# Stored input product of the r and z gates added on TensorE instead of VectorE, in a GRU followed by routed experts

## The chip, the cores and the metric

The kernel runs on one core of a Trainium2 chip. The metric is the device time of one execution, in microseconds (us). PE is TensorE (products; PEld its weight loads), DVE is VectorE, ACT is ScalarE, POOL is GpSimd, SP issues most transfers.

## The reference

A GRU with 512 units runs over 512 time steps for 4 sequences; its states are the input of a two-of-four mixture of experts, and the result is added to x. In the excerpt the expert part is cut, since the change does not touch it.

```python
def cell(h, x):
    gi = x @ W_ih + b_ih
    gh = h @ W_hh + b_hh
    i_r, i_z, i_n = jnp.split(gi, 3, axis=-1)
    h_r, h_z, h_n = jnp.split(gh, 3, axis=-1)
    r = jax.nn.sigmoid(i_r + h_r)
    z = jax.nn.sigmoid(i_z + h_z)
    n = jnp.tanh(i_n + r * h_n)
    h_new = (1.0 - z) * n + z * h
    return (h_new, h_new)
...
_, hs = jax.lax.scan(cell, initial_state, xs)
...
x = x + _L0_ffn_ref(hs, Wg, bg, W1, W2)
```

## The kernel before

**Segments.** Each sequence is cut into 16 segments of L = 32 steps, so 4 x 16 = 64 columns (COLS) run side by side. The start of a segment is found by running the 40 steps ahead of it from zero: 8 steps (BURN) on the end of the segment before the last one, then 32 on the last one. After 8 and after 40 steps the states are shifted by one segment (L985 `shift`), and the first column gets the true initial state. Then 32 steps follow whose states are kept. That makes FIRST + L = 72 steps. A test on DVE (L1053 `check`) compares each segment's end with the start that the next one assumed; if the largest gap is above 2^-20 of the largest state, all engines run 32 steps more, up to 15 times.

**Numbers.** Weights and states are scaled by powers of two and split into an fp16 high half and an fp16 low half. The first 20 steps (ROUGH) multiply high by high only: 4 k-tiles x 4 units x 3 gates = 48 products of 128x128 by 128x64. The other 52 are exact and take high x high, high x low weight and low state x high: 144 products. A "unit" j is one of four blocks of 128 hidden units; its three gates r, z, n lie in PSUM bank j.

**The input product** gi = x W_ih is made in four chunks of 8 steps. The first is made before step 0 in fp32 (L319, 12 tiles in 4 banks, each emptied by ACT at L545 or L548). The other three are made beside the steps, as "fills": 18 split products of 512 columns (L336) per step in steps 0 to 23 (FILLED), 1.5 tiles a step, emptied by ACT (L554) into fp32 in SBUF. The order in a rough step is 13 fills, the first k-tile, 2 fills, and so on (FILLS). From step 24 on a step has no fills.

**One step.** PE waits for the high half of state tile k (`high_ready`) and, once per unit, until the bank is read (`rn_done`). For each unit DVE adds the r and z part of gi to PSUM (L934 `pre_rz`), ACT takes one sigmoid of both (L582), POOL forms z h (L720), DVE forms r (h_n + b) (L939 `reset`), adds i_n (L944), ACT takes tanh (L587), DVE forms (z - 1) n (L948), then the new state's high half (L955 `blend`) and, again in fp32, the state itself (L960, L965). In exact steps POOL forms the low halves 0 to 2 (L728), DVE the last one (L970). The orders are written out by hand: `ORDER` (L225) for PE, `exact` and `rough` (L972, L976) for DVE, L589 for ACT. Between steps DVE also splits x and W_hh (L878, L925), one piece per step.

**Start-up.** DVE takes maxima of W_ih (L854), x (L862) and W_hh (L884), POOL reduces them over partitions (L702 to L708), DVE makes power-of-two scales of them (L840 `pow2`), ACT and DVE split W_ih (L528, L873). The first six tiles are kept unscaled and multiplied later (L909).

## Time and profile before

| what | value |
|---|---|
| runs, us | 954.76, 973.03, 952.18 |
| median, us | 954.76 |
| the profiled execution, us | 953.15 |
| its span, first to last instruction, us | 951.4 |
| granted PE clock, mean over the span | 0.955 |
| busy share PE, DVE, ACT, POOL | 84%, 70%, 44%, 21% |

The span is one profiled execution; it is 1.75 us shorter than that execution's own time. A timeline row has its start, its length from the first start to the last end, engine, line, operation, what is written and read, the number of instructions merged into it, and in brackets the idle time before it with what ended it. A "mean ns" of a product is its own latency; products overlap, so rates are taken from starts.

### The profile page before, as it was taken

To read this page: it belongs to the slowest core of one execution; us is meant where nothing else is said; L and a number is where in the kernel's file an instruction comes from. 1 tells how busy PE (TensorE), PEld (TensorE's weight loads), DVE (VectorE), ACT (ScalarE), POOL (GpSimd) and SP (SyncE) were. 2 spreads that over 40 slices of the span, in tenths; PEclk is the share of its full clock that TensorE was granted. 3 is DMA by queue.
4 is the path that set the end of the run, shared out by engine and by line. 5 is a ranking of instruction groups with operands and counts; after the bars stand their busy time and mean duration, and the time that the engine had idled before them with its cause. 6 is when DMAs were issued, how large, how long until landed. Compare 5 with 4: busy or idle time off the path is not lost.

```text
span 951.4 us, 27392 instructions
## 1 busy us (share of the span) xinstructions
PE 798.6 (84%) x11202; PEld 516.0 (54%) x11203; DVE 664.7 (70%) x2254; ACT 419.8 (44%) x844; POOL 195.8 (21%) x507
## 2 busy tenths in 40 slices
PE   6998788998888688887884514899999999999996
PEld 2444444577777677777774513444444444444442
DVE  5867777767888788888885586567765767575500
ACT  1656455654444344444442330574175418334700
POOL 1012111233333333333331001001201210210011
PEclk9999999999999999999997855999999999999999
DMA  9700000000000000000002274053525523370012
GB/s 346 273 2 2 1 2 2 2 3 3 4 3 4 2 4 3 4 3 4 4 3 90 91 221 165 14 180 85 167 61 171 154 67 132 90 208 12 1 18 27
DMA packets 20162, 62.52 MB, mean 66 GB/s; under 512 B 2064, under 2 KB 2064, under 8 KB 17424
## 3 DMA queue, kind: packets, MB, share of 16 engines
q1 hardware_dynamic: 15744, 52.46, 15.8%
q0 software_dynamic: 3584, 8.42, 5.0%
q8 instruction: 81, 1.33, 0.6%
q14 instruction: 33, 0.27, 0.1%
q10 hardware_dynamic: 720, 0.03, 0.0%
HBM read 52.49 MB, written 12.62 MB: 68 GB/s over the span
## 4 chain that ended last, share of the span: by engine, by line
PE 69%; DVE 20%; issue 5%; ACT 4%; DMA 1%; POOL 0%; DVEq 0%; POOLq 0%; SPq 0%; ACTq 0%
PE ps L344 21%; PE ps L486 17%; PE ps L499 17%; DVE wa L934 5%; PE ps L319 5%; DVE wa L939 4%; PE ps L336 3%; DVE wa L944 3%; DVE halves L955 3%; PE ps L428 2%; DVE ocand L948 2%; ACT wa L582 2%; PE ps L466 1%; DMA big<-in_w_ih 1%; PE ps L474 1%
## 5 line engine op out<-in xcount | busy, mean ns | idle before, releaser
L344 PE MATMUL ps<-halves,wa 128*128 128x64 f16 x8448 | 292.0, 194 | 76.6 <-DVE halves L955 66.4
L344 PEld LDWEIGHTS ps<-halves,wa 128*128 128x128 f16 x8448 | 272.2, 98 | 115.7 <-DVE wa L939 56.3
L582 ACT ACTIVATE wa<-wa,un_gates 128x128 f32<-128x128 f32 x288 | 112.6, 398 | 163.5 <-DVE wa L934 155.1
L486 PE MATMUL ps<-wb,big 128*128 128x512 f16 x768 | 166.9, 379 | 1.6 <-DVE wb L1246 1.6
L499 PE MATMUL ps<-big 128*128 128x512 f16 x768 | 166.9, 379 | 0.0
L486 PEld LDWEIGHTS ps<-wb,big 128*128 128x128 f16 x768 | 74.8, 98 | 91.6 <-issue 1.8
L587 ACT ACTIVATE wa<-wa,un_gates 128x64 f32<-128x64 f32 x288 | 94.1, 343 | 67.9 <-DVE wa L944 65.6
L499 PEld LDWEIGHTS ps<-big 128*128 128x128 f16 x768 | 75.2, 98 | 89.9
L934 DVE TENSOR_TENSOR wa<-ps,big 128x128 f32<-128x128 f32 x288 | 81.1, 287 | 54.0 <-PE ps L344 54.0
L336 PE MATMUL ps<-hx,wb 128*128 128x512 f16 x432 | 109.8, 386 | 0.0
L647 ACT ACTIVATE hx<-ps,un_hid_in 128x512 f32<-128x512 f32 x64 | 43.7, 683 | 112.5 <-PE ps L486 110.2
L720 POOL TENSOR_TENSOR wa<-wa,carried 128x64 f32<-128x64 f32 x160 | 52.3, 331 | 167.8 <-ACT wa L582 165.5
L955 DVE SCALAR_TENSOR_TENSOR halves<-ocand,neg_scale,wa 128x64 f16<-128x64 f32 x288 | 80.8, 280 | 8.4 <-issue 0.6
L939 DVE SCALAR_TENSOR_TENSOR wa<-ps,bhn_s,wa 128x64 f32<-128x64 f32 x288 | 80.0, 278 | 5.6 <-ACT wa L582 5.5
L1138 DVE SCALAR_TENSOR_TENSOR big<-wa,scale,big 128x2048 f16<-128x2048 f32 x28 | 65.3, 2349 | 25.9 <-ACT big L633 25.9
L633 ACT ACTIVATE big<-wa,scale 128x2048 f16<-128x2048 f32 x32 | 62.5, 1989 | 44.6 <-DVEq L1126 44.6
L1259 DVE SCALAR_TENSOR_TENSOR big<-hx,hid_scale,big 128x512 f16<-128x512 f32 x64 | 47.9, 749 | 42.8 <-ACT big L650 36.6
L944 DVE TENSOR_TENSOR wa<-wa,big 128x64 f32<-128x64 f32 x288 | 69.7, 242 | 2.5
L1097 DVE TENSOR_REDUCE chunk_peak<-wa 128x1 f32<-128x2048 f32 x32 | 71.1, 2276 | 0.0
L948 DVE SCALAR_TENSOR_TENSOR ocand<-wa 128x64 f32<-128x64 f32 x288 | 62.8, 218 | 10.9 <-ACT wa L587 10.9
L720 POOL TENSOR_TENSOR wa<-wa,hx 128x64 f32<-128x64 f32 x128 | 41.4, 323 | 88.0 <-ACT wa L582 84.4
L778 POOL DMA_INDIRECT out<-hx,idx_out x16 | 29.1, 1818 | 136.1 <-DVE hx L1265 136.1
(168 smaller groups left out, 610.9 us busy)
## 6 DMA issues: line engine op xcount, KB each, us to landing
wa<-in_w SPq DMA_DIRECT2D x32, 1024.0 KB, 7.7
hs_rows<-big SPq DMA_DIRECT2D x8, 516.0 KB, 6.3
big<-in_w_ih SPq DMA_DIRECT2D x3, 1024.0 KB, 11.3
hx<-in_x_t SPq DMA_DIRECT2D x3, 1024.0 KB, 20.0
big<-in_w_hh SPq DMA_DIRECT2D x4, 768.0 KB, 16.4
wa<-in_x_t SPq DMA_DIRECT2D x1, 1024.0 KB, 4.9
hx<-hs_rows,idx POOLq DMA_INDIRECT x16
out<-hx,idx_out POOLq DMA_INDIRECT x16, 4.9
```

What stands on the lines that cost most here:

```text
L336: mm = pe.matmul(ps[:, 4 + tile % 4, :], wih_parts[:, w, k, m * P:(m + 1) * P], x_parts[:, q, t, k, :], start=(left == 0), stop=(left == K ...
L344: mm = pe.matmul(gate_ps[:, j, g, :], whh_parts[:, k, w, (4 * g + j) * P:(4 * g + j + 1) * P], halves[:, src, k, h, :], start=(k == 0 and ...
L486: mm = pe.matmul(ps[:, m % 2, :], w1p[:, w, k, m * P:(m + 1) * P], tokT[:, t, k, :], start=(k == 0 and n == 0), stop=(k == KD - 1 and n == 2))
L499: mm = pe.matmul(ps[:, 2 + g % 2, :], hid[:, h, k, g * P:(g + 1) * P], w2p[:, w, k, :], start=(k == 0 and n == 0), stop=(k == KH - 1 and n ...
L582: act.activation(rz[:, j, :, :], pre[:, j, :, :], ACT.Sigmoid, scale=un_gates[:, 0:1]).then_inc(S["sig_done"], 1)
L587: act.activation(cand[:, j, :], cand_in[:, j, :], ACT.Tanh, scale=un_gates[:, 0:1]).then_inc(S["tanh_done"], 1)
L720: pool.tensor_tensor(zh[:, j, :], rz[:, j, 1, :], before(j), ALU.mult).then_inc(S["zh_done"], 1)
L934: dve.tensor_tensor(pre[:, j, :, :], gate_ps[:, j, 0:2, :], gi_rz(j), ALU.add).then_inc(S["pre_ready"], 1)
L939: dve.scalar_tensor_tensor(rn[:, j, :], gate_ps[:, j, 2, :], bhn_s[:, j:j + 1], rz[:, j, 0, :], ALU.add, ALU.mult).then_inc(S["rn_done"], 1)
L944: dve.tensor_tensor(cand_in[:, j, :], rn[:, j, :], gi_n(j), ALU.add).then_inc(S["candin_ready"], 1)
L948: dve.scalar_tensor_tensor(ocand[:, j, :], rz[:, j, 1, :], -1.0, cand[:, j, :], ALU.add, ALU.mult).then_inc(S["ocand_done"], 1)
L955: dve.scalar_tensor_tensor(halves[:, dst, j, HIGH, :], ocand[:, j, :], neg_scale[:, 0:1], zh[:, j, :], ALU.mult, ALU.add).then_inc(S["high ...
```

## The change

PE now adds the r and z part. ACT empties a tile of those gates, with bias and scaled to fit fp16, into a ring of three fp32 buffers (`gi_full`); a cast makes its high half and a subtraction on DVE its low half (`rz_high`, `rz_low`; in the first chunk ACT does the cast). Both lie where the fp32 tile lay. At a unit's start PE multiplies a diagonal matrix (bf16, a power of two, `diag`) with 128 columns of the high half, in exact steps also of the low half (`inject`), then the recurrent products accumulate. ACT takes its sigmoid straight from PSUM once the unit is complete. `pre_rz` is gone, its buffer too.

With it: the two shifts before step 8 and step 40 are no longer copies; the last step before each writes its halves and states one segment further (`moved`), and the first column is written in that step. In rough steps the state is no longer kept in fp32; z h uses the high half. In exact steps DVE forms low halves 2 and 3, POOL 0 and 1, and states are kept unit by unit. The first product's tiles wait for the scales, which now also cover the bias and the first chunk of x. The splits of x come one step later, and those of W_hh stand at steps 5 to 8 and 13 to 15 (`WHH_AT`: two in each of 5 to 8 and 13, one in 14 and 15). PE's and DVE's orders are new.

```diff
+        INJECT = 2
+        ORDER = ((INJECT, 0, 0), (INJECT, 1, 0), (HIGH, 1, 0), (INJECT, 2, 0), (HIGH, 0, 0), (HIGH, 2, 0),
...
+        LOW_BY = "PPDD"
...
+        TILES = tuple((CHUNK_ORDER[0], m) for m in range(12)) + tuple(
+            (c, 4 * g + j) for c in CHUNK_ORDER[1:] for j in range(KD) for g in range(3))
...
+        def split_by(i):
+
+            return 12 + 3 * (i + (i % STEPS_C == STEPS_C - 1)) // 2
...
+            def inject(j, c, cols, parts, steps):
+
+                pe.wait_ge(S["rn_done"], steps + j + 1)
+                for part in parts:
+                    pe.matmul(gate_ps[:, j, 0:2, :], diag[:, 1 if c in (1, 2) else 0, :], gi_rz[:, c, j, part, :, cols],
+                              start=(part == HIGH), stop=False, skip_group_check=True)
...
+                        pe.wait_ge(S["gi_high"], 8 * (i // STEPS_C) + 8)
                     pe.wait_ge(S["high_ready"], made(i) + k + 1)
                     for j in range(KD):
                         if k == 0:
-
-                            pe.wait_ge(S["rn_done"], KD * i + j + 1)
+                            inject(j, *place(i), (HIGH,), KD * i)
                         unit(HIGH, j, k, src, (HIGH,), k == KD - 1)
 
...
+                    if h == INJECT:
+                        inject(j, c, cols, (HIGH, LOW), steps)
+                        continue
...
+            pe.wait_ge(S["diag_ready"], 1)
...
+                if i < FILLED:
+                    fill(FILL_STEP * i, FILL_STEP * i + FILL_STEP)
+                if i == ROUGH:
+                    pe.wait_ge(S["gi_low"], 8 * 3)
+                if i == FILLED:
+                    pe.wait_ge(S["gi_high"], 8 * NC_)
+                    pe.wait_ge(S["gi_low"], 8 * NC_)
+                gates(i % 2, *place(i), made(i), lows(i), KD * i)
...
+            def keep_tile(t, q, sc, g_sc):
+
+                c, m = TILES[t]
+                act.wait_ge(S["gi_mm"], t + 1)
+                if m < 8:
+                    if rz_count(t) >= GI_RING:
+                        act.wait_ge(S["gi_low"], rz_count(t) - GI_RING + 1)
+                    act.activation(gi_full[:, rz_count(t) % GI_RING, :], ps[:, 4 + t % 4, :], ACT.Identity,
+                                   bias=bias_gi[:, q, m:m + 1], scale=sc).then_inc(S["gi_kept"], 1)
+                else:
+                    act.activation(gi[:, c, m % 4, 2, :], ps[:, 4 + t % 4, :], ACT.Identity, bias=bsum_g[:, m:m + 1],
+                                   scale=g_sc).then_inc(S["gi_kept"], 1)
...
+                keep_tile(m, 0, gi_scale[:, 0:1], gates_scale[:, 0:1])
+                if m < 8:
+                    act.wait_ge(S["gi_kept"], m + 1)
+                    rz_high(m)
...
                 def sig(j):
-                    act.wait_ge(S["pre_ready"], base + j + 1)
-                    act.activation(rz[:, j, :, :], pre[:, j, :, :], ACT.Sigmoid,
+                    act.wait_ge(S["gates_mm"], base + j + 1)
+                    act.activation(rz[:, j, :, :], gate_ps[:, j, 0:2, :], ACT.Sigmoid,
                                    scale=un_gates[:, 0:1]).then_inc(S["sig_done"], 1)
...
+                if i < ROUGH:
+                    return lambda j: halves[:, i % 2, j, HIGH, :]
+                if i < FIRST:
+                    return lambda j: carried[:, i % 2, j, :]
+                return lambda j: hs[:, j, i - FIRST, :]
...
+            dve.wait_ge(S["x_loaded"][0], 16)
+            dve.tensor_reduce(chunk_peak[:, 3:4], x_first, AX.XY, ALU.max, apply_absolute_value=True
...
             dve.wait_ge(S["peak_known"], 1)
+            link(dve.tensor_scalar(peak_all[:, WIH:WIH + 1], peak_all[:, WIH:WIH + 1], 1e-30, None, ALU.max))
+            link(dve.reciprocal(bias_room[:, :], peak_all[:, WIH:WIH + 1]))
+            link(dve.scalar_tensor_tensor(bias_room[:, :], peak_all[:, BIAS:BIAS + 1], BIAS_TO, bias_room[:, :],
+                                          ALU.mult, ALU.mult))
+            link(dve.tensor_tensor(peak_all[:, X0:X0 + 1], peak_all[:, X0:X0 + 1], bias_room[:, :], ALU.max))
             pow2(slice(WIH, X0 + 1))
...
+                link(dve.scalar_tensor_tensor(gi_scale[:, q:q + 1], scale[:, WIH:WIH + 1], GI_TO,
+                                              scale[:, X0 if q == 0 else X1:(X0 if q == 0 else X1) + 1],
+                                              ALU.mult, ALU.mult))
+                link(dve.tensor_scalar(bias_gi[:, q, :], bsum[:, 0:8], gi_scale[:, q:q + 1], None, ALU.mult))
+
+            gi_scales(0)
             dve.sem_inc(S["x_known"], 1)
...
+            def rz_high(t):
+
+                c, m = TILES[t]
+                dve.wait_ge(S["gi_kept"], t + 1)
+                dve.tensor_copy(gi_rz[:, c, m % 4, HIGH, m // 4, :], gi_full[:, rz_count(t) % GI_RING, :]
+                                ).then_inc(S["gi_high"], 1)
+
+            def rz_low(t):
+
+                c, m = TILES[t]
+                dve.wait_ge(S["gi_high"], rz_count(t + 1))
+                dve.tensor_tensor(gi_rz[:, c, m % 4, LOW, m // 4, :], gi_full[:, rz_count(t) % GI_RING, :],
+                                  gi_rz[:, c, m % 4, HIGH, m // 4, :], ALU.subtract).then_inc(S["gi_low"], 1)
+
+            for m in range(4):
+                rz_low(m)
...
-            for m in range(SCALED):
-                dve.wait_ge(S["gi_ready"], m + 1)
-                dve.tensor_scalar(gi[:, CHUNK_ORDER[0], m % 4, m // 4, :], gi[:, CHUNK_ORDER[0], m % 4, m // 4, :],
-                                  gates_scale[:, 0:1], None, ALU.mult).then_inc(S["first_scaled"], 1)
             dve.wait_ge(S["peak_known"], 3)
...
+            link(dve.tensor_tensor(peak_all[:, X1:X1 + 1], peak_all[:, X1:X1 + 1], bias_room[:, :], ALU.max))
             pow2(slice(X1, X1 + 1))
+            gi_scales(1)
...
+            for q in range(2):
+                ins = dve.tensor_scalar(diag[:, q, :], ident[:, :], un_gi[:, q:q + 1], 1.0 / GI_TO, ALU.mult, ALU.mult)
+            link(ins)
+            dve.sem_inc(S["diag_ready"], 1)
             dve.sem_inc(S["gi_known"], 1)
...
+                def low_part(j):
+                    dve.wait_ge(S["state_done"], base + (j + 1 - KD * (ROUGH - 1)))
+                    whole = hs[:, j, 0, :] if moved else after(j)
+                    dve.tensor_tensor(halves[:, dst, j, LOW, :], whole, halves[:, dst, j, HIGH, :], ALU.subtract
+                                      ).then_inc(S["last_low_ready"], 1 + (POOL_LOWS if j == KD - 1 else 0))
+                exact = ((reset, 0), (candidate_in, 0), (reset, 1), (candidate_in, 1), (reset, 2),
...
+                rough = ((reset, 0), (candidate_in, 0), (reset, 1), (candidate_in, 1), (one_less_z, 0), (reset, 2),
...
+                         (one_less_z, 2), (blend, 2), (one_less_z, 3), (blend, 3), (other_work, 0))
...
+                moved = i in (BURN - 1, FIRST - 1)
...
+                between = []
+                if i < FILLED:
+                    for t in range(split_by(i - 1), split_by(i)):
+                        if TILES[t][1] < 8:
+                            between += [(rz_high, t), (rz_low, t)]
+                if 1 <= s <= KD and q < 2:
+                    between.append((x_low, (q + 1, s - 1)))
+                for n in WHH_AT.get(i, ()):
+                    between.append((whh_low, n))
+                step(lambda j, c=c, cols=cols: gi[:, c, j, 2, cols], after, i % 2, KD * i, i >= ROUGH - 1, moved, between)
```

On PE, the start of an exact step without fills. L344 is a recurrent product; each group of six is one unit and one state tile. Before:

```order
L344 MATMUL ps<-halves,wa 128x64 [waits high_ready,rn_done]
L344 MATMUL ps<-halves,wa 128x64 x5
L344 MATMUL ps<-halves,wa 128x64 [waits rn_done]
L344 MATMUL ps<-halves,wa 128x64 x5
L344 MATMUL ps<-halves,wa 128x64 [waits rn_done]
L344 MATMUL ps<-halves,wa 128x64 x5
L344 MATMUL ps<-halves,wa 128x64 [waits rn_done]
L344 MATMUL ps<-halves,wa 128x64 x5
L344 MATMUL ps<-halves,wa 128x64 [waits high_ready]
L344 MATMUL ps<-halves,wa 128x64 x23
```

and now, with L386 the injection and L376 the recurrent product:

```order
L386 MATMUL ps<-big,diag 128x128 [waits rn_done]
L386 MATMUL ps<-big,diag 128x128
L386 MATMUL ps<-big,diag 128x128 [waits rn_done]
L386 MATMUL ps<-big,diag 128x128
L376 MATMUL ps<-halves,wa 128x64 [waits high_ready]
L376 MATMUL ps<-halves,wa 128x64 x5
L386 MATMUL ps<-big,diag 128x128 [waits rn_done]
L386 MATMUL ps<-big,diag 128x128
L376 MATMUL ps<-halves,wa 128x64 x12
L386 MATMUL ps<-big,diag 128x128 [waits rn_done]
L386 MATMUL ps<-big,diag 128x128
L376 MATMUL ps<-halves,wa 128x64 [waits high_ready]
```

The injections of units 0 and 1 stand ahead of the wait for the high half of state tile 0, those of units 2 and 3 behind it, and the first recurrent products are those of unit 1.

On DVE, the start of the same step. Before, with L934 the sum of r and z, L939 the reset, L944 the candidate's input, L948 (z - 1) n, L955 the high half:

```order
L934 TENSOR_TENSOR wa<-ps,big 128x128 x2
L939 SCALAR_TENSOR_TENSOR wa<-ps,bhn_s,wa 128x64
L934 TENSOR_TENSOR wa<-ps,big 128x128
L944 TENSOR_TENSOR wa<-wa,big 128x64
L939 SCALAR_TENSOR_TENSOR wa<-ps,bhn_s,wa 128x64
L944 TENSOR_TENSOR wa<-wa,big 128x64
L934 TENSOR_TENSOR wa<-ps,big 128x128
L948 SCALAR_TENSOR_TENSOR ocand<-wa 128x64
L939 SCALAR_TENSOR_TENSOR wa<-ps,bhn_s,wa 128x64
L955 SCALAR_TENSOR_TENSOR halves<-ocand,neg_scale,wa 128x64
L948 SCALAR_TENSOR_TENSOR ocand<-wa 128x64
L944 TENSOR_TENSOR wa<-wa,big 128x64
```

and now, with L1047, L1052, L1056 and L1063 for the last four, and L1068 for the state in fp32:

```order
L1047 SCALAR_TENSOR_TENSOR wa<-ps,bhn_s,wa 128x64
L1052 TENSOR_TENSOR wa<-wa,big 128x64
L1047 SCALAR_TENSOR_TENSOR wa<-ps,bhn_s,wa 128x64
L1052 TENSOR_TENSOR wa<-wa,big 128x64
L1047 SCALAR_TENSOR_TENSOR wa<-ps,bhn_s,wa 128x64
L1056 SCALAR_TENSOR_TENSOR ocand<-wa 128x64
L1052 TENSOR_TENSOR wa<-wa,big 128x64
L1063 SCALAR_TENSOR_TENSOR halves<-ocand,neg_scale,wa 128x64
L1068 SCALAR_TENSOR_TENSOR hx<-ocand,neg_scale,wa 128x64
L1056 SCALAR_TENSOR_TENSOR ocand<-wa 128x64
L1047 SCALAR_TENSOR_TENSOR wa<-ps,bhn_s,wa 128x64
```

The four sums are gone, the candidate of unit 2 now follows (z - 1) n of unit 0, and the state of unit 0 is kept right behind its high half, ahead of reset 3.

On DVE in the start-up, from POOL's first answer on. Before, four operations made the scales, and the maximum of W_hh followed:

```order
L843 TENSOR_SCALAR peak_all<-peak_all 128x2
L844 TENSOR_SCALAR unscale<-peak_all 128x2
L846 TENSOR_SCALAR scale<-unscale 128x2
L848 TENSOR_SCALAR unscale<-unscale 128x2
L884 TENSOR_REDUCE chunk_peak<-big 128x1
L873 SCALAR_TENSOR_TENSOR wb<-big,scale,wb 128x1536
```

and now, with L946 and L949 the scale and the scaled bias of the tiles and L965 the low halves of the first four tiles:

```order
L937 TENSOR_SCALAR peak_all<-peak_all 128x1
L938 RECIPROCAL bias_room<-peak_all 128x1
L939 SCALAR_TENSOR_TENSOR bias_room<-peak_all,bias_room 128x1
L941 TENSOR_TENSOR peak_all<-peak_all,bias_room 128x1
L909 TENSOR_SCALAR peak_all<-peak_all 128x2
L910 TENSOR_SCALAR unscale<-peak_all 128x2
L912 TENSOR_SCALAR scale<-unscale 128x2
L914 TENSOR_SCALAR unscale<-unscale 128x2
L946 SCALAR_TENSOR_TENSOR gi_scale<-scale 128x1
L949 TENSOR_SCALAR bias_gi<-bsum,gi_scale 128x8
L965 TENSOR_TENSOR big<-gi_full,big 128x512 x4
L985 TENSOR_REDUCE chunk_peak<-big 128x1
```

Four linked operations stand ahead of the scales, two behind them, and four subtractions that need ACT's tiles stand ahead of the maximum of W_hh.

## Rows read from the trace of the kernel before

**Rows 1.** The page: busy time of each engine, and one of its costliest groups.

```profile
PE 798.6 (84%) x11202; PEld 516.0 (54%) x11203; DVE 664.7 (70%) x2254; ACT 419.8 (44%) x844; POOL 195.8 (21%) x507
...
L344 PE MATMUL ps<-halves,wa 128*128 128x64 f16 x8448 | 292.0, 194 | 76.6 <-DVE halves L955 66.4
```

**Rows 2.** Chain that ended last, in one exact step: start, length, what.

```profile
263.76 2.29 PE ps L344 x69
...
266.05 1.33 PE ps L344 x36
...
269.60 0.42 PE ps L344 x9
```

**Rows 3.** Timelines of DVE and of ACT in the same exact step.

```profile
266.88 0.29 DVE L934 TENSOR_TENSOR wa<-ps,big 128x128 f32<-128x128 f32 x1 [0.36 <-PE ps L344]
...
267.64 0.28 DVE L939 SCALAR_TENSOR_TENSOR wa<-ps,bhn_s,wa 128x64 f32<-128x64 f32 x1
...
268.05 0.21 DVE L944 TENSOR_TENSOR wa<-wa,big 128x64 f32<-128x64 f32 x1
...
269.18 0.28 DVE L955 SCALAR_TENSOR_TENSOR halves<-ocand,neg_scale,wa 128x64 f16<-128x64 f32 x1
...
267.20 1.36 ACT L582 ACTIVATE wa<-wa,un_gates 128x128 f32<-128x128 f32 x3 [1.87 <-DVE wa L934]
268.48 0.62 ACT L587 ACTIVATE wa<-wa,un_gates 128x64 f32<-128x64 f32 x2
```

**Rows 4.** Timeline of PE: rough, filled and exact steps, idle time in brackets.

```profile
56.65 0.51 PE L344 MATMUL ps<-halves,wa 128*128 128x64 f16 x12
...
168.20 0.72 PE L344 MATMUL ps<-halves,wa 128*128 128x64 f16 x12 [0.35 <-DVE halves L955]
...
186.15 0.73 PE L344 MATMUL ps<-halves,wa 128*128 128x64 f16 x12 [0.31 <-DVE halves L955]
...
188.84 4.05 PE L336 MATMUL ps<-hx,wb 128*128 128x512 f16 x18
192.72 4.36 PE L344 MATMUL ps<-halves,wa 128*128 128x64 f16 x144
196.92 4.05 PE L336 MATMUL ps<-hx,wb 128*128 128x512 f16 x18
...
222.50 2.67 PE L344 MATMUL ps<-halves,wa 128*128 128x64 f16 x76 [1.16 <-DVE halves L955]
...
502.78 4.73 PE L344 MATMUL ps<-halves,wa 128*128 128x64 f16 x144 [1.10 <-DVE halves L955]
```

**Rows 5.** Timelines of PE, ACT and DVE over the start-up.

```profile
9.50 44.51 PE L319 MATMUL ps<-wa,big 128*128 128x512 f32 x96 [9.50 <-DMA big<-in_w_ih]
...
26.58 0.69 ACT L545 ACTIVATE big<-ps,bsum 128x512 f32<-128x512 f32 x1 [2.75 <-PE ps L319]
...
34.17 2.55 ACT L539 ACTIVATE hx<-hx,scale 128x512 f16<-128x512 f32 x4
...
19.13 2.28 DVE L862 TENSOR_REDUCE peak<-hx 128x1 f32<-128x2048 f32 x1
...
23.22 0.17 DVE L843 TENSOR_SCALAR peak_all<-peak_all 128x2 f32<-128x2 f32 x1 [1.44 <-POOL peak_all L702]
...
28.76 1.82 DVE L873 SCALAR_TENSOR_TENSOR wb<-big,scale,wb 128x1536 f16<-128x1536 f32 x1 [2.99 <-ACT wb L528]
...
42.80 2.74 DVE L878 SCALAR_TENSOR_TENSOR hx<-hx,scale 128x512 f16<-128x512 f32 x4
...
50.02 2.47 DVE L909 TENSOR_SCALAR big<-big,gates_scale 128x512 f32<-128x512 f32 x6 [0.16 <-DVE peak L904]
...
53.28 0.23 DVE L915 TENSOR_SCALAR un_gi<-un_gi,gates_scale 128x2 f32<-128x2 f32 x1
```

**Rows 6.** PE's timeline at step 8, and granted clock (1.00 is full) from 110 to 157 us.

```profile
111.79 0.82 PE L344 MATMUL ps<-halves,wa 128*128 128x64 f16 x12 [4.29 <-DVEq L993]
...
110.00:157.00 47.00, 38.66 (x410) 21.81 (x411) 33.02 (x145) 23.21 (x59) 7.92 (x24) 0.89 0.00 1
```

More of the change, by code:

```diff
@@ L982, in step, with shift @@
+                for n, (f, j) in enumerate(exact if low else rough):
+                    f(j)
+                    if moved and n == 0:
+                        first_column(low)
                 if low:
-                    last_low(KD - 1)
-            def shift(count, ends, starts, starts_all, low):
+                    other_work(0)
+            def shift(count, ends, starts, starts_all):
                 for k in range(KD):
```

287 lines of the change are left out of this document (139 added, 148 removed).

## The prediction

> **What bounds the kernel now.** Read the page's first part, then its costliest groups. PE is busy 84% of the span and DVE 70% [rows 1], but that averages three kinds of work: a start-up, 72 GRU steps, then routing and experts, which the change does not touch. The group of L344 counts 8448 recurrent products; 20 rough steps of 48 and 52 exact steps of 144 make exactly that, so one pass of 72 steps was enough.
>
> Next, the chain that ended last, cut to one exact step in the middle [rows 2]. It starts on PE at 263.76 us and again at 269.60, so a step takes 5.84 us. PE works 69 + 36 products before the chain leaves it; the step ends on DVE, and PE restarts on the high half of unit 0. So the loop is: products of the first units, sigmoid, reset, candidate, tanh, blend, back to PE.
>
> The timelines of DVE and ACT in the same step [rows 3] show how the time after PE is spent. Unit 0's sum with the stored input product (L934) starts at 266.88, its sigmoid at 267.20, the reset (L939) at 267.64, its candidate (L944) at 268.05, tanh at 268.48, the high half (L955) at 269.18, landing 269.46, and PE starts 0.14 later. From 266.88 to 269.60 are 2.72 us, and from PE's start to 266.88 another 3.12.
>
> How fast PE is when nothing makes it wait stands in the steps that carry fills [rows 4]: 144 products from 192.72 to 196.92 are 4.20 us, 29.2 ns apart; 18 fills of 512 columns from 188.84 to 192.72 are 216 ns apart. An exact step thus holds 4.20 us of PE work in 5.84: it is a latency loop, not PE's rate. Rough steps hold 18 x 0.216 + 48 x 0.0292 = 5.29 us and take (186.15 - 168.20)/3 = 5.98 late in the run, but (186.15 - 56.65)/19 = 6.82 on average.
>
> **The exact step.** Removed: four L934 sums on DVE (0.29 us each, 0.21 to the next start) and one handover. Added: eight products of 128 columns; four of them (units 0 and 1) stand ahead of the wait for the high half and run while PE waits. The price of 128 columns is not shown. By the line through 29.2 ns at 64 and 216 at 512 columns it is 56 ns; the bounds are 29 and 216. I take 56, since the line joins the two nearest sizes.
>
> PE's part: in the new order gate 0 is complete after 81 products and 4 injections, 2.37 + 0.22 us, plus 0.16 until its result can be used and 0.08 for a restart: 2.83.
>
> After it, with gate 0 complete at 0.00 and gates 1 and 2 at 0.44 and 0.79 (15 and 27 products on): sigmoids at 0.03, 0.47, 0.82 (0.40 each); reset 0 at 0.46, candidate 0 at 0.84 (0.28 and about 0.1 to hand over); reset 1 at 0.98, candidate 1 at 1.36, reset 2 at 1.50; tanh 0 stands behind sigmoid 2 and runs 1.13 to 1.48; one-minus-z at 1.70, candidate 2 at 1.88, the high half at 2.02, landing 2.30; PE starts at 2.42. Sum 5.25 us. The same recurrence with the old order gives 5.80, against 5.84 in the trace. In the new step halves 2 and 3 of the low parts land 4.8 to 4.9 us after gate 0 and PE wants them at 4.8 to 4.9, without margin; for that I take 5.30.
>
> Bounds: 5.1 if the injections and handovers are cheap, 5.5 if PE keeps 0.3 us of stalls, which is what the old step has (3.12 less 87 x 0.0292 and 0.2 to finish).
>
> From step 24 to step 71 are 47 periods, 502.78 - 222.50 = 280.3 us, of which 47 x 5.84 = 274.3 and 6.0 for the second shift and short disturbances. After: 47 x 5.30 = 249.1, plus 0.6 for the two linked first-column copies in step 39 and 1.0 kept for disturbances. **Term: -29.6.** The last step's DVE work ends, by the same two recurrences, 7.6 instead of 8.6 after PE's start: **-1.0.**
>
> **Rough steps.** DVE loses its four sums and its state copies and gains one tile per step to split: a cast and a subtraction of 512 columns. A one-input operation of 512 columns takes 2.47/6 = 0.41 us, a two-input one 2.74/4 = 0.68 [rows 5]; together 1.1. DVE's own 16 instructions end about 3.0 us after gate 0, the next reset is wanted at 5.9, so 1.1 plus one or two weight splits of 0.68 lie beside PE's fills. PE then bounds: 5.29 + 4 x 0.056 = 5.51, taken 5.55. Step 8 and step 16 wait for the last tile of the chunk just made, whose cast stands in the previous step's tail: 1.7 each. The shift at step 8, where PE stood 4.29 us [rows 6], goes. 19 x 5.55 + 3.4 = 108.9 against 129.5. **Term: -20.6.**
>
> **Filled steps and step 24.** From step 19's products to step 24's were 222.50 - 186.15 = 36.35 us. After: 2.7 + 4 x (3.89 + 4.20 + 0.45) = 36.9. Step 24 now waits for every low half of the input product: after the last tanh of step 23 come ACT's tile, then on DVE the step's own tail and two cast-and-subtract pairs of 1.1; they end about 7.0 after gate 0, and PE, done at 1.84, restarts at 7.1: 5.3 us idle. **Term: +5.9.**
>
> **Start-up.** Here the change costs. Before, PE ran its first product without a break, 44.51 us from 9.50, and went straight on [rows 5]; ACT emptied the first banks unscaled, at 26.58 the fourth. Now ACT waits until the scale is known. That was after the four small operations from 23.22, 0.8; it gains a 2.28 us maximum, two small steps (0.4) and six linked ones (1.2): about 27.7. Then ACT needs 4 x 1.25 for the first four tiles and their halves before it may split W_ih, which it had begun when the fourth bank was empty, at about 27.2: +5.7. DVE, which stood 2.99 us for that half at 28.76, comes out 6.6 later; three more low halves bring 8.6, a fourth waits for ACT and makes 9.4. The six rescalings go (2.47), but they had hidden POOL's answer, 1.8 from request to use (1.44 of it idle at 23.22); with its three links and the two diagonals DVE is ready at about 63.1 where it was at 53.5. PE waits for the diagonals before its first fill: **+9.3.** It stands idle 5.7 us before them. After the 4.29 us at step 8 the granted clock was 0.89 over the next 47 us [rows 6], so part of the work there ran at 1.2 GHz; two such places: **+1.0.**
>
> Sum: 9.3 + 1.0 - 20.6 + 5.9 - 29.6 - 1.0 = -35.0. The profiled execution took 953.15 us, so 918.1; the median of the runs lies 1.6 above it. I say 919.
>
> **A rule weighed.** Between the rows' two sizes the spacing grows with the columns, which gave 56 ns. The Trainium skill, "TensorE: Matmul & The Clock Gate", section "Back-to-back issue gap", says that a sustained stream of weight loads and products of 128 columns comes at some 81 ns each. The rows here show less than that at 64 columns (29.2 ns), and no row has 128. By 81, with 4 exposed per exact step and all eight or four elsewhere, the sum would be 7 us higher.
>
> **The rivals.**
> *PE keeps starving.* The low halves 2 and 3, both on DVE now behind four state copies, come late and each step waits 0.25 more: 5.55, or 930. For it: no margin in the schedule. Against: only the end of the loop's PE part is hit.
> *Cheaper than reckoned.* Period 5.0 and the wait at step 24 shared with the filled work: 903. For it: PE's bare work is 4.65. Against: sigmoid 2 still stands before tanh 0.
> *Rough steps become DVE's.* If cast, subtraction and splits delay the resets, they stay at 6.8 and lose 20: 939. For it: two weight splits fall into steps 5 to 8 and 13, 2.5 us of extra work there with the tile. Against: 1.0 us of sums per step leaves, and 3 us lie between the last blend and the next reset.
> *The product does not pipeline.* If an injected product costs its whole 0.19 us [rows 1], 0.14 more, with 4 exposed in 48 exact steps, 8 in the 4 filled and 4 in 20 rough ones, that is 27 + 4 + 11 = 42 more: 961, no gain. For it: another weight type and a two-part access. Against: 144 products of 64 columns overlap fully.
> *A second pass* (the slower side). DVE compares the segment ends with the assumed starts; above 2^-20 of the largest state, all engines run 32 more exact steps and the test. Twenty rough steps now carry the state itself in fp16 and use only the high half of the input product, so their error is larger; 20 exact steps follow to damp it. Price 32 x 5.3 + 11: 1100. It decides at that threshold alone. Against: the old rough steps already rounded weights and state to fp16, and one pass sufficed [rows 1].
>
> **How the numbers follow.** Forecast (905 to 930) 0.60, starving 0.15, cheaper 0.10, DVE-bound 0.07, no pipelining 0.04, second pass 0.04. Range: the period's bounds give -9 and +9, start-up and step 24 together 5 either way, the rough steps 5; with both neighbours 902 to 940. Two per cent is 19 us, about what a measurement can tell from no change (the runs span 952 to 973): faster needs under 936. That takes the forecast, cheaper, starving and a little of the DVE-bound case: 0.86; same 0.10; slower 0.04.
>
> **What would show it.** Right: PE's starts of step 24 onwards 5.2 to 5.4 us apart; rough starts 5.5 to 5.6; one gap of 5 to 6 us on PE before its first fill and one at step 24; no gap at steps 8 and 40 beyond 2 us; 72 steps. Wrong: L386 over 70 ns apart, resets late in the rough steps, or more than 8448 recurrent products.

## The result, and the profile after

| | before | after |
|---|---|---|
| median of 4 runs, us | 954.65 (952.18 to 973.03) | 914.84 (913.26 to 918.5) |
| ratio to before, 95% interval | | 0.9597 (0.9552 to 0.9641) |
| profiled execution, us; its span | 953.15; 951.4 | 913.26; 911.5 |

One of the four runs before (973.03 us) was in a slower state of the chip and is left out of the ratio, which for that reason is not 914.84/954.65. The forecast was 919 us, within 902 to 940. From the profile's page of the changed kernel: its busy line and three of its costliest groups (line, engine, operation, tiles, shapes, count; busy us, mean ns of one; idle before, and what ended most of it).

```profile
PE 810.2 (89%) x11698; PEld 533.4 (59%) x11699; DVE 634.6 (70%) x2087; ACT 414.3 (45%) x852; POOL 178.2 (20%) x454
...
L376 PE MATMUL ps<-halves,wa 128*128 128x64 f16 x8448 | 290.6, 194 | 7.9 <-DVE halves L1063 1.6
...
L648 ACT ACTIVATE wa<-ps,un_gates 128x128 f32<-128x128 f32 x288 | 100.1, 365 | 139.0 <-PE ps L376 132.5
L386 PE MATMUL ps<-big,diag 128*128 128x128 f16 x496 | 62.8, 221 | 10.9 <-DVE big L958 10.9
```

L376 is the recurrent product, L344 of [rows 1]: again 8448, so one pass. L386 is the injection (the new product that adds the r and z input product to PSUM). L648 is the sigmoid, which now reads PSUM. PE is busy 89% instead of 84%: the same other work in a shorter span, plus the injections. PE lost idle time in the exact steps and in most rough ones. Four gaps are left, which its timeline shows (start us, us, operation, count, and in brackets the idle time ahead of it and what ended it); the one of 3.38 us is at step 8, where the kernel before had 4.29 [rows 6]:

```profile
60.85 5.00 PE L368 MATMUL ps<-hx,wb 128*128 128x512 f16 x13 [4.92 <-DVEq L1022]
65.68 0.22 PE L386 MATMUL ps<-big,diag 128*128 128x128 f16 x1
...
113.30 0.29 PE L386 MATMUL ps<-big,diag 128*128 128x128 f16 x1 [3.38 <-DVE big L958]
...
161.28 0.23 PE L386 MATMUL ps<-big,diag 128*128 128x128 f16 x1 [2.40 <-DVE big L958]
...
177.81 0.22 PE L386 MATMUL ps<-big,diag 128*128 128x128 f16 x1
...
219.96 0.58 PE L386 MATMUL ps<-big,diag 128*128 128x128 f16 x4 [5.16 <-DVE big L958]
220.34 0.53 PE L376 MATMUL ps<-halves,wa 128*128 128x64 f16 x6
...
221.73 5.51 PE L376 MATMUL ps<-halves,wa 128*128 128x64 f16 x126
...
463.30 0.35 PE L376 MATMUL ps<-halves,wa 128*128 128x64 f16 x6
```

These rows bound the stages: the first unit of step 0 starts at 65.68, of step 19 at 177.81, of step 24 at 220.34, of step 71 at 463.30. L958 is the cast of a tile of the input product to its high half. The first gap waits for the diagonals, the other three for the last tile of a chunk of eight steps. Behind three of the four PE runs at half clock: the granted clock is 0.50 from 60.8 to 64.0, from 113.3 to 115.0 and from 219.9 to 224.0, and 1.00 behind the gap of 2.40 (full clock is 2.4 GHz, 0.50 is 1.2). At half clock 13 fills take 5.00 us (2.97 in other steps) and step 24's 126 products 5.51 (3.87 in other steps). Against [rows 4]:

| stage | before, us | after, us | measured | forecast |
|---|---|---|---|---|
| up to step 0's products | 56.65 | 65.68 | +9.0 | +9.3 |
| 19 rough steps | 129.5 | 112.1 | -17.4 | -20.6 |
| step 19 to step 24 | 36.35 | 42.5 | +6.2 | +5.9 |
| 47 exact steps | 280.3 | 243.0 | -37.3 | -29.6 |
| step 71 to the end | 448.6 | 448.2 | -0.4 | -1.0 |
| clock, not tied to a stage | | | in the stages | +1.0 |
| sum | 951.4 | 911.5 | -39.9 | -35.0 |

An exact step in the middle, as the chain of waits has it (start us, us, what the chain lies on; "issue" is a handover), where [rows 2] has 5.84 us:

```profile
253.20 0.35 PE ps L376 x6
253.55 0.11 PE ps L386 x2
253.66 0.35 PE ps L376 x12
254.01 0.11 PE ps L386 x2
254.12 1.98 PE ps L376 x63
...
256.12 0.38 ACT wa L648
...
256.52 0.29 DVE wa L1047
...
256.84 0.23 DVE wa L1052
...
257.72 0.13 DVE ocand L1056
257.85 0.06 DVE wa L1052
257.91 0.04 issue
257.95 0.30 DVE halves L1063
258.25 0.05 issue
258.30 0.35 PE ps L376 x6
```

From PE's restart at 253.20 to the next at 258.30 are 5.10 us. PE's part ends at 256.10, after 2.90; the rest is 2.20: sigmoid, resets (L1047), candidates (L1052, the later ones left out), z-1 times n (L1056), high half (L1063). Two injections take 0.11, so 56 ns each, which was the estimate. The sum on DVE (L934 in [rows 3]) is gone, and ACT's sigmoid follows PE directly.

Where the chain leaves PE has changed too. Before, it left after 105 products (69 + 36 in [rows 2]), with unit 1 complete, and these lines of the same chain follow:

```profile
267.40 0.29 DVE wa L934
267.70 0.23 DVE wa L939
267.93 0.21 DVE wa L934
```

DVE had unit 1's sum ahead of unit 0's reset (L939), and two more sums in the chain up to the high half. From PE's start to 267.38 are 3.62 us, and 2.22 followed. Now the chain leaves PE after 81 products, at 2.90, and 2.20 follow. Followed along unit 0, as the prediction does, the same step is 3.12 + 2.72 before and 2.92 + 2.18 after.

### The profile page after: what moved, and what is told of

Read it like the earlier page. It is cut to its first block, busy times and chain, and to the rows that moved or that the text cites. A ratio compares the mean times of both kernels' runs of the same rounds, so it can differ in the third digit from the quotient of the medians.

```text
span 911.5 us, 28124 instructions
## 1 busy us (share of the span) xinstructions
PE 810.2 (89%) x11698; PEld 533.4 (59%) x11699; DVE 634.6 (70%) x2087; ACT 414.3 (45%) x852; POOL 178.2 (20%) x454
## 4 chain that ended last, share of the span: by engine, by line
PE 69%; DVE 20%; issue 4%; ACT 3%; DMA 1%; POOL 0%; DVEq 0%; ACTq 0%; POOLq 0%
PE ps L376 18%; PE ps L538 18%; PE ps L551 18%; PE ps L368 8%; DVE wa L1047 4%; DVE wa L1052 3%; DVE halves L1063 3%; ACT wa L648 2%; PE ps L480 2%; PE ps L386 2%; DVE ocand L1056 1%; PE ps L518 1%; PE ps L526 1%; DMA bg_sb<-in_bg 1%; DVE big L965 1%
## 5 line engine op out<-in xcount | busy, mean ns | idle before, releaser
L376 PE MATMUL ps<-halves,wa 128*128 128x64 f16 x8448 | 290.6, 194 | 7.9 <-DVE halves L1063 1.6
L376 PEld LDWEIGHTS ps<-halves,wa 128*128 128x128 f16 x8448 | 274.2, 98 | 35.4 <-DVE halves L1063 15.9
L648 ACT ACTIVATE wa<-ps,un_gates 128x128 f32<-128x128 f32 x288 | 100.1, 365 | 139.0 <-PE ps L376 132.5
L1047 DVE SCALAR_TENSOR_TENSOR wa<-ps,bhn_s,wa 128x64 f32<-128x64 f32 x288 | 80.2, 278 | 72.2 <-ACT wa L648 72.2
L653 ACT ACTIVATE wa<-wa,un_gates 128x64 f32<-128x64 f32 x288 | 99.1, 344 | 57.5 <-DVE wa L1052 51.1
L1063 DVE SCALAR_TENSOR_TENSOR halves<-ocand,neg_scale,wa 128x64 f16<-128x64 f32 (+1 forms) x288 | 86.8, 301 | 4.5 <-issue 0.5
L386 PE MATMUL ps<-big,diag 128*128 128x128 f16 x496 | 62.8, 221 | 10.9 <-DVE big L958 10.9
L1052 DVE TENSOR_TENSOR wa<-wa,big 128x64 f32<-128x64 f32 x288 | 66.0, 229 | 5.1
L1056 DVE SCALAR_TENSOR_TENSOR ocand<-wa 128x64 f32<-128x64 f32 x288 | 62.6, 217 | 0.1
L368 PEld LDWEIGHTS ps<-hx,wb 128*128 128x128 f16 x432 | 38.5, 99 | 40.8 <-DVEq L1022 5.7
```

Source lines behind the costliest of these rows:

```text
L368: mm = pe.matmul(ps[:, 4 + tile % 4, :], wih_parts[:, w, k, m * P:(m + 1) * P], x_parts[:, q, t, k, :], start=(left == 0), stop=(left == K ...
L376: mm = pe.matmul(gate_ps[:, j, g, :], whh_parts[:, k, w, (4 * g + j) * P:(4 * g + j + 1) * P], halves[:, src, k, h, :], start=False, stop= ...
L386: pe.matmul(gate_ps[:, j, 0:2, :], diag[:, 1 if c in (1, 2) else 0, :], gi_rz[:, c, j, part, :, cols], start=(part == HIGH), stop=False, s ...
L648: act.activation(rz[:, j, :, :], gate_ps[:, j, 0:2, :], ACT.Sigmoid, scale=un_gates[:, 0:1]).then_inc(S["sig_done"], 1)
L653: act.activation(cand[:, j, :], cand_in[:, j, :], ACT.Tanh, scale=un_gates[:, 0:1]).then_inc(S["tanh_done"], 1)
L1047: dve.scalar_tensor_tensor(rn[:, j, :], gate_ps[:, j, 2, :], bhn_s[:, j:j + 1], rz[:, j, 0, :], ALU.add, ALU.mult).then_inc(S["rn_done"], 1)
```

## The experiments

Each ran beside the kernel before on the same chip; ratios are to it. The quoted expectations were on record before each run.

**1. The sum stays on DVE.** `e3`: L386 is taken out, and DVE adds the stored high half to PSUM ahead of the sigmoid; the low half is left out, and DVE's order has the sums ahead of the resets.

```diff
-                for part in parts:
-                    pe.matmul(gate_ps[:, j, 0:2, :], diag[...], gi_rz[:, c, j, part, :, cols], ...)
+                def pre_rz(j):
+                    dve.wait_ge(S["gates_mm"], base + j + 1)
+                    dve.scalar_tensor_tensor(pre[:, j, :, :], gi_pre(j), pre_sc[:, q:q + 1], gate_ps[:, j, 0:2, :],
+                                             ALU.mult, ALU.add).then_inc(S["pre_ready"], 1)
```

> The changed kernel with the sum of r and z back on DVE, ahead of the resets as in the old order of DVE, and no injections; everything else of the change stays (tiles as fp16 halves, states moved by offset writes, low halves 2 and 3 on DVE, unit order of PE). The low half of the input product is left out of the sum. Theory that the injection makes the gain of the exact steps: they return to 5.9 or 6.0 us, +41 in 48 steps, less 6 for PE in filled and rough steps: about 950. Rival, the gain comes from the other edits: 5.3 at most and 925.

Measured: 992.52 us, ratio 1.0397 (1.0374 to 1.042). Timeline of PE in its exact steps:

```profile
254.62 1.29 PE L378 MATMUL ps<-halves,wa 128*128 128x64 f16 x30 [1.29 <-DVE halves L1068]
256.14 3.50 PE L378 MATMUL ps<-halves,wa 128*128 128x64 f16 x114 [0.23 <-POOL halves L793]
260.72 1.29 PE L378 MATMUL ps<-halves,wa 128*128 128x64 f16 x30 [1.08 <-DVE halves L1068]
```

The step is 6.10 us, 1.0 more than after, as the theory had it (5.9 to 6.0 forecast); the rival, a gain from the other edits, is out. The total missed by 42 us: the forecast had the sums free in the rough steps. They are not: with them PE stands idle 0.4 to 1.3 us in most rough steps too (4.69 us ahead of step 16), and of the 80 us of span between this kernel and the changed one (991.3 and 911.5) only 47 lie in the 47 exact steps. One part is this form's own: its sum, which reads fp16 halves and scales them, takes 0.34 us, where the one before took 0.29 [rows 3]. So taking the sum off DVE is what lets the rough steps run at PE's rate, as well as what shortens the exact ones. With the sum in this form the other edits alone would lose time.

**2. PE's order without injections.** `e5`: the kernel before, with the changed kernel's sequence of products.

```diff
-        ORDER = ((HIGH, 0, 0), (HIGH, 1, 0), (HIGH, 2, 0), (HIGH, 3, 0), (HIGH, 1, 1), (HIGH, 3, 1),
+        ORDER = ((HIGH, 1, 0), (HIGH, 0, 0), (HIGH, 2, 0),
+                 (HIGH, 0, 1), (HIGH, 1, 1), (LOW, 1, 0), (HIGH, 2, 1), (LOW, 2, 0),
```

> The kernel before with one thing taken from the change: its 32 products of a step stand in the order of the changed kernel (unit 0 first, unit 2 ahead of unit 3's last ones); no input product is added to PSUM, the sums and sigmoids of r and z stay as they were. Theory (the gain of 37 us in the exact steps comes from taking the sums of r and z out of the chain of the recurrence, and the order only serves the injections): the exact step stays at 5.84 us or gets up to 0.05 longer, the time is 952 to 960 us. Rival (the order starts the high halves of unit 0 early enough that it alone takes 0.1 to 0.3 us from each of 47 exact steps): 940 to 950 us.

Measured: 957.37 us, ratio 1.0037 (1.0019 to 1.0055). As the theory had it: the exact step is 5.88 us, the order alone gains nothing, and PE's timeline now lists 0.17 us of idle time for a low half on POOL in each step, where it listed none before.

```profile
257.07 1.21 PE L344 MATMUL ps<-halves,wa 128*128 128x64 f16 x30 [0.99 <-DVE halves L955]
258.45 3.50 PE L344 MATMUL ps<-halves,wa 128*128 128x64 f16 x114 [0.17 <-POOL halves L728]
```

**3. The old order with injections.** `e2`: in the changed kernel, the products stand as in the kernel before, the injections of a unit ahead of its first.

```diff
-        ORDER = ((INJECT, 0, 0), (INJECT, 1, 0), (HIGH, 1, 0), (INJECT, 2, 0), (HIGH, 0, 0), (HIGH, 2, 0),
+        ORDER = ((INJECT, 0, 0), (INJECT, 1, 0),
+                 (HIGH, 0, 0), (HIGH, 1, 0), (INJECT, 2, 0), (HIGH, 2, 0), (INJECT, 3, 0), (HIGH, 3, 0),
```

> The changed kernel with the recurrent products of exact steps in the old order (unit 0 first, gate 1 complete after 105 products), injections ahead of each unit. Latency theory, by the recurrence of the prediction with the durations now measured: 5.33 a step, +11: 926. Rival, the order of products is worth nothing since the sum of work is the same: 5.10 and 915.

Measured: 924.72 us, ratio 0.9682 (0.9666 to 0.9698); the exact step 5.26 us (251.61 to 256.87). With the injections the order is worth 0.16 us per step: 0.06 until unit 0's sigmoid, 0.10 until its high half, because unit 1's gate comes later. Less than the 0.23 expected.

**4. Injections moved behind the wait.** `e1`: the four injections of units 0 and 1 wait for the new state too.

```diff
+                pe.wait_ge(S["high_ready"], base + 1)
                 for h, j, k in ORDER:
```

> The changed kernel, in exact steps PE waits for the high half of state tile 0 ahead of the injections of units 0 and 1 too. Latency theory: an exact step is a loop that PE's work does not bound, and these four injections (56 ns each) run in PE's idle time; exposed, they lengthen every exact step by 0.22 us, from 5.10 to 5.32, and 48 steps make +10.6: about 925. Rival, PE's work bounds the step: the work is the same, so 5.10 and 915 stay.

Measured: 921.44 us, ratio 0.9648 (0.9627 to 0.9669); the exact step 5.20 us. Four products of 56 ns are 0.22, but the step grew by 0.10. The cover is real, its price was wrong, and the next two runs look for the missing 0.12. In the trace step 71 starts 7.2 us later than in the changed kernel: 4.5 are the 47 steps, and 2.7 are there at step 24 already, ahead of the steps that the edit touches most; they are half clock that lasted longer behind the same gaps.

**5. and 6. Four more injections, early or late.** `e8` and `e9`: the low half is added three times for two of the four units.

```diff
-                        inject(j, c, cols, (HIGH, LOW), steps)
+                        inject(j, c, cols, (HIGH, LOW, LOW, LOW) if j in (0, 1) else (HIGH, LOW), steps)
```

(`e9` has units 2 and 3 in place of 0 and 1.)

> The changed kernel with four more injections in each exact step: the low half of the input product of units 0 and 1 is added three times instead of once (so these sums are other numbers), in the place where the injections of these units stand, in front of the products that wait for the new state. Theory (the exact step is set by the recurrence, and TensorE has some 0.26 us idle just after these injections): 4 x 56 ns = 0.22 us fit into that idle time, the exact step stays at 5.09 to 5.12 us and the time at 913 to 918 us; the rough steps have high halves only and don't change. Rival (TensorE is the bound, every instruction added to it is paid): 0.22 us x 47 = 10.5 us more, some 925 us, as with the four at the other units.

> The changed kernel with four more injections in each exact step, at units 2 and 3: the low half of the input product of these units is added three times instead of once (so these sums are other numbers). These injections stand among the products that start once the new state is there. Theory (what TensorE does after the state has come and before unit 0's sigmoid is in the chain of the recurrence): 4 x 56 ns = 0.22 us is paid in each of 47 steps, the exact step goes from 5.10 to 5.32 us and the time to 923 to 928 us. Rival (an injection overlaps the products around it and costs next to nothing wherever it stands): 914 to 917 us.

Measured: `e8` 917.66 us, ratio 0.9627 (0.9605 to 0.9648), exact step 5.09 us; step 71 starts 0.8 us later, a difference that is there by step 24. `e9` 920.99 us, ratio 0.9653 (0.9631 to 0.9675), exact step 5.20; its step 71 starts 7.8 us later, 3.3 of them by step 24. So in front of the wait injections are free, as the prediction had it, and behind it four of them cost 0.10, not 0.22. Timelines of PE in one step of the changed kernel:

```profile
253.85 0.28 PE L386 MATMUL ps<-big,diag 128*128 128x128 f16 x2
254.06 3.87 PE L376 MATMUL ps<-halves,wa 128*128 128x64 f16 x126
```

and of `e9`:

```profile
252.53 0.39 PE L386 MATMUL ps<-big,diag 128*128 128x128 f16 x4
252.76 3.84 PE L376 MATMUL ps<-halves,wa 128*128 128x64 f16 x126
```

Read the starts, not the lengths. In the changed kernel two injections are followed after 0.21 us, in `e9` four are followed after 0.23. Two should take 0.11: PE waits 0.10 in the first case for something, and no row lists it, because a product is in flight for 0.19 us and covers it. What PE needs there is the high half of unit 1; DVE's timeline of the changed kernel ends it at 254.00:

```profile
253.59 0.41 DVE L1063 SCALAR_TENSOR_TENSOR halves<-ocand,neg_scale,wa 128x64 f16<-128x64 f32 x1
```

Extra injections ahead of that point fill this wait before they lengthen the step: 0.22 - 0.10 = 0.12, near the 0.10 measured.

**7. and 8. The hidden wait itself.** `e10` writes unit 0's full state behind unit 1's high half; `e11` puts unit 2's injections in front of the wait for the state.

```diff
-                         (one_less_z, 0), (candidate_in, 2), (blend, 0), (keep_state, 0), (one_less_z, 1),
-                         (reset, 3), (blend, 1), ...
+                         (one_less_z, 0), (candidate_in, 2), (blend, 0), (one_less_z, 1),
+                         (reset, 3), (blend, 1), (keep_state, 0), ...
```

```diff
-        ORDER = ((INJECT, 0, 0), (INJECT, 1, 0), (HIGH, 1, 0), (INJECT, 2, 0), (HIGH, 0, 0), (HIGH, 2, 0),
+        ORDER = ((INJECT, 0, 0), (INJECT, 1, 0), (INJECT, 2, 0), (HIGH, 1, 0), (HIGH, 0, 0), (HIGH, 2, 0),
```

> The changed kernel with one VectorE instruction of each exact step moved: the full state of unit 0 is written behind the high half of unit 1 instead of ahead of it. Theory (the four extra injections in front of or behind the state cost 0.10 us instead of 0.22 because TensorE waits another 0.10 us for the high half of unit 1, behind unit 3's injections, which the records don't list as idle): the high half of unit 1 comes 0.2 us earlier, this wait goes, and the exact step takes 4.99 to 5.01 instead of 5.10 us, 909 to 911 us. The low half of unit 0 comes 0.4 us later on GpSimd and is read 0.5 us after it came so far. Rival (there is no such wait, the step is TensorE's instructions and VectorE's chain alone): 5.09 to 5.11, 914 to 916 us.

> The changed kernel with the two injections of unit 2 put with those of units 0 and 1, ahead of the wait for the new state, so that six of eight lie in TensorE's idle time. Theory (the hidden wait for unit 1's high half ends at the same moment after the state as before, so what is saved ahead of it is waited for there): exact step 5.09 to 5.10 us, 913.5 to 917 us. Rival (each injection behind the new state is paid with 56 ns, as the prediction's sum has it): 5.10 - 0.11 = 4.99 us, 909 to 911 us.

Measured: `e10` 915.87 us, ratio 0.9594 (0.9578 to 0.961); `e11` 916.53 us, ratio 0.9592 (0.9575 to 0.961). `e11` is as the theory had it: two injections moved out of the way, nothing gained. For `e10` the time is the rival's, but the timeline of PE, and below it the one of POOL, show why:

```profile
254.22 0.28 PE L386 MATMUL ps<-big,diag 128*128 128x128 f16 x2
254.33 3.97 PE L376 MATMUL ps<-halves,wa 128*128 128x64 f16 x126
```

```profile
254.39 0.35 POOL L794 TENSOR_TENSOR halves<-carried,halves 128x64 f16<-128x64 f32 x1 [0.39 <-DVE carried L1068]
```

The 0.10 after the injections is gone (254.22 to 254.33), so it was a wait for unit 1's high half. But the 126 products now take 3.97 instead of 3.87. The low half of unit 0 leaves POOL at 254.74, 1.17 us after this step's restart at 253.57. In the changed kernel it is 0.72 after the restart (253.92, 253.20), so it comes 0.45 later, as expected. PE wants it after 12 more products, at 254.33 + 12 x 0.029 = 254.68, which was 254.41 in the changed kernel: 1.11 after the restart and not 1.21. So the slack of 0.49 us is used up by the 0.45 and by the 0.10 that was to be gained, and with the handover from POOL the same 0.10 is waited for there. The second chain of the step came to be as long as the first.

**9. The wait for the diagonals.** `e4`: PE waits for them and for w_hh ahead of the first injection, not ahead of the first fills.

```diff
                     if k == 0 and i % STEPS_C == 0:
+                    if k == 0 and i == 0:
+                        pe.wait_ge(S["diag_ready"], 1)
+                        pe.wait_ge(S["whh_high"], KD)
...
-            pe.wait_ge(S["diag_ready"], 1)
-            pe.wait_ge(S["whh_high"], KD)
```

> The changed kernel, PE waits for the diagonals only ahead of the first injection, behind the first 13 fills. Theory that the start-up loss is this wait and the half clock behind it: fills run from 56 to 59 at full clock, the first injection comes at 60.9 where it came at 65.7: -4.8, about 910. Rival, the fills themselves wait for DVE's splits: the first injection stays near 64 to 66 and 915 stays.

Measured: 909.06 us, ratio 0.9514 (0.9498 to 0.9529). Timeline of PE:

```profile
56.57 2.96 PE L368 MATMUL ps<-hx,wb 128*128 128x512 f16 x13 [0.65 <-ACT big L605]
60.84 0.23 PE L386 MATMUL ps<-big,diag 128*128 128x128 f16 x1 [1.30 <-DVEq L1023]
...
108.56 0.29 PE L386 MATMUL ps<-big,diag 128*128 128x128 f16 x1 [3.38 <-DVE big L959]
...
218.08 0.58 PE L386 MATMUL ps<-big,diag 128*128 128x128 f16 x4 [5.16 <-DVE big L959]
```

The fills run in 2.96 us, the first injection comes 4.84 us earlier, step 8's 4.74, but step 24's only 1.88. The medians show more, 5.8 us, but this profiled execution (911.21, granted clock 0.947) is the longest of its four (the others 0.951 to 0.953) and that of the changed kernel the shortest; only the trace's 1.9 is accounted for, and whether the other executions gave anything back is not shown. The gaps at 8 and 16 are as long as before (3.38 and 2.39). What grew is the step behind each: 8.08 and 7.15 us instead of 6.86 and 5.51, against 5.51 for a step at full clock.

**10. The r and z tiles first.** `e6`: the chunk's tiles are computed gate by gate.

```diff
-            (c, 4 * g + j) for c in CHUNK_ORDER[1:] for j in range(KD) for g in range(3))
+            (c, 4 * g + j) for c in CHUNK_ORDER[1:] for g in range(3) for j in range(KD))
```

> The changed kernel with one line changed: of each chunk of eight steps the input product's tiles of gates r and z are computed and stored ahead of those of the candidate, instead of unit by unit over all three gates. The injections of a chunk's first step read the r and z tiles, the candidate's tile is read later. Theory (the gaps of 3.38, 2.40 and 5.16 us at steps 8, 16 and 24 are TensorE waiting for the last r and z tile of the chunk to be converted to halves, and the half clock that follows each of them costs some 1.4, 0 and 2.2 us): with these tiles ready earlier at least 8 of the 11 us of gaps and most of the half clock go, the first injection of step 24 comes 10 to 13 us earlier, 901 to 906 us. Rival (VectorE's and ScalarE's work for the tiles is the pace of the stage, so the wait only moves to the candidate's tile, as when the start-up was made 4.8 us shorter and 3 us of them were given back): 910 to 915 us.

Measured: 902.17 us, ratio 0.9462 (0.9442 to 0.9483). Timeline of PE:

```profile
110.67 0.22 PE L386 MATMUL ps<-big,diag 128*128 128x128 f16 x1 [0.38 <-issue]
...
208.78 0.39 PE L386 MATMUL ps<-big,diag 128*128 128x128 f16 x4
209.31 0.35 PE L376 MATMUL ps<-halves,wa 128*128 128x64 f16 x6
```

Step 24's first injection comes 11.2 us earlier with no gap before it, step 8's gap is 0.38, and the step after step 24 is at full clock. The tiles' work was not the pace; only the order in which they were needed was.

**11. Both stage edits.** `e7` is `e4` and `e6` together.

> The changed kernel with two edits together: the r and z tiles of a chunk first, and TensorE's wait for the diagonals and for w_hh behind the first fills instead of ahead of them. With the second edit alone the first injection came 4.84 us earlier but 3 us of it were given back until step 24, because the half clock behind the gaps at steps 8 and 16 lasted longer (8.08 and 7.15 us for a step instead of 6.86 and 5.51). Theory (with the gaps gone there is nothing left that gives it back): 4.2 to 4.9 us less than with the tiles alone (902.17), 897 to 898.5 us, and step 24's first injection at 199 to 200 us of the span instead of 204.1. Rival (VectorE's and ScalarE's work on the tiles is the pace of this stage): the injection at step 24 stays at 203 to 204 us and the time at 901 to 903 us.

Measured: 898.19 us, ratio 0.9412 (0.9396 to 0.9428), the fastest here. Step 24's injection comes at 205.00 against 208.78: with no gaps behind it, 3.8 of the 4.5 us by which its first injection comes earlier (60.60 against 65.12) are kept, and the medians differ by 4.0. (The 199 to 200 us expected went by the row at 204.1 of `e6`, which is step 23's.)

**12. All four edits.** `e12` is `e7` with the edits of `e10` and `e11`.

> The changed kernel with all four edits: r and z tiles first, the wait for the diagonals behind the first fills, unit 0's full state behind unit 1's high half, unit 2's injections ahead of the wait for the new state. Theory: with the wait for unit 1's high half gone, the third pair of injections in the idle time pays too; exact step 5.10 - 0.10 - 0.11 = 4.89 us, 47 x 0.21 = 10 us below the version with the two stage edits: 886 to 890 us. Rival (something else is late next, a low half of GpSimd or TensorE's idle time used up): 4.95 to 5.00 us, 891 to 894 us.

Measured: 898.47 us, ratio 0.9404 (0.9389 to 0.942), no gain over `e7`, and neither expectation. The exact step is 5.09. Its chain of waits runs the other way round:

```profile
256.85 0.28 DVE halves L1064
...
257.74 0.21 DVE carried L1069
...
258.01 0.37 POOL halves L795
258.38 0.05 issue
258.43 0.58 PE ps L376 x14
```

The step now goes through unit 0's full state on DVE and its low half on POOL, the chain that `e10` had made as late as the first.

## Why the prediction was right, and where its terms were off

**The mechanism of the exact step held.** It stayed a latency loop; the sum left it (run 1: 1.0 us per step comes back with it); injections in front of the wait are hidden (run 5). The forecast called PE's idle time the cover and priced a product of 128 columns at 56 ns; the chain shows 0.11 for two. The rule of the Trainium skill's page "TensorE: Matmul & The Clock Gate", section "Back-to-back issue gap", some 81 ns each for a sustained stream, does not fit the injections: with their weight loads they come at 56 to 57 ns. They come here in twos and fours, up to eight in run 5 (0.45 us), and no run has a longer stream of them.

**Its size was off by 7.7 us: "for that I take 5.30".** The ordinary step is 5.10. The recurrence itself gave 5.25, and 0.05 were added for low halves that do not hold PE up here (126 products in 3.87). In the recurrence, PE's part measured 2.90 against 2.83, because of the hidden 0.10 of run 7. The part behind it measured 2.20 against 2.42: the sigmoid from PSUM takes 0.38 and not 0.40, and each handover on DVE 0.02 to 0.04, where 0.1 was taken between reset and candidate and 0.12 for PE's restart (0.14 in [rows 3]), which is now 0.05. Of the 47 x 0.20 = 9.4 us, 1.7 went back: 3.3 us of the stage are not ordinary steps, against 1.6 kept. The half clock in step 24 alone is 2.15 (7.25 us from first product to first product, 220.34 to 227.59).

**Rough steps: the period right, the two waits too small.** The ordinary rough step is 5.51 us against 5.55, at PE's rate, as reckoned. "1.7 each" for steps 8 and 16 measured 3.38 and 2.40. The timeline of DVE in the changed kernel, from the last high half of step 7 on:

```profile
111.56 0.28 DVE L1063 SCALAR_TENSOR_TENSOR halves<-ocand,neg_scale,wa 128x60 f16<-128x60 f32 x1
111.76 0.42 DVE L958 CAST big<-gi_full 128x512 f16<-128x512 f32 x1
112.21 0.69 DVE L965 TENSOR_TENSOR big<-gi_full,big 128x512 f16<-128x512 f32 x1
112.82 0.42 DVE L958 CAST big<-gi_full 128x512 f16<-128x512 f32 x1
```

Ahead of the cast that PE waits for stand another tile's cast and its subtraction, 1.06 us that the forecast had put into the step before. Another 1.35 us is step 8's half clock.

**Start-up and step 24 were right** (+9.0 for +9.3; +6.2 for +5.9), the first partly by two errors that cancel: DVE was ready 2.3 us earlier than reckoned (60.8, not 63.1), since POOL's first answer was waited for 0.30 us and not 1.44, and its last came 0.55 us after the request and not 1.8, and the 13 fills after the gap ran 2.0 us slower.

**The clock term was too small.** +1.0 was taken; the four gaps cost 2.0, 1.35, 0 and 2.15 us in the steps behind them, 5.5 in all. The 2.0 are in the start-up, which for that reason looked right, 1.35 in the rough steps and 2.15 in the exact ones. No row gave the 1.0: the one it named, 0.89 over 47 us, is 5.2 us short of full clock, idle time included. Run 10 shows it from the other side: without the gaps the granted clock from 110 us to 300 us is 1.00 in each stretch.

**The signs.** Of the forecast's own signs of being right, three came out otherwise: starts 5.10 apart (5.2 to 5.4), a first gap of 4.92 us (5 to 6) and 3.38 at step 8 (no more than 2). None of its signs of being wrong came. Its last sum is rounded low: 918.1 and 1.6 make 919.7, where it says 919.

**The rivals.** "Cheaper than reckoned" came half true: the period of 5.10 lies between the forecast's 5.30 and its 5.0, but the wait at step 24 was paid in full (5.16 us). PE did not starve, the rough steps did not become DVE's, the product pipelines, and there was no second pass.

So the total was within 0.5% by a mechanism that was right, but its two largest terms were off by 7.7 and 3.2 us in opposite directions.

## What to carry to other kernels

Moving an addition from a busy engine into PSUM costs TensorE a short product for each stored half, and that product is free where TensorE already waits for the next state; issue it in front of the wait. Before counting that gain as final, look at what else the new form makes wait: here the same edit made the first step of each chunk need every r and z tile, and ordering the tiles by need (one line) gave another 13 us. When an edit should have gained and did not, compare the start times of neighbouring rows with the unit spacing: two chains of equal length hide each other, and shortening one of them shows nothing.

## What the runs showed of the hardware that was not expected

- A wait of PE that is over before the 0.19 us for which the last product is in flight have passed appears in no list of waits. It is seen only in the starts: 0.21 us after two products of 56 ns, 0.11 in run 7. The kernel before shows it too: 144 products took 4.36 us behind fills and 4.73 in an ordinary exact step, with nothing listed inside [rows 4].
- The price of a gap on PE is not fixed by its length. Behind a gap of 3.38 us the same step took 6.86 us in the changed kernel and 8.08 in `e4`, behind one of 2.40 or 2.39 us 5.51 and 7.15. In the profiled execution of `e4` 3 us of the 4.84 were given back in this way. The edit need not be the cause: behind the same gap of 4.92 us and the same start-up the 13 fills took 5.00 us in the changed kernel, 5.73 in `e1`, 4.92 in `e8`, 4.42 in `e9` and 4.29 in `e6`. What sets it was not tried.
- Two to eight products of 128 columns in a row, with their weight loads, came at 56 to 57 ns each, between 29.2 at 64 columns and 216 at 512, on the straight line that the prediction had drawn.
